# Router logits of an attention and mixture-of-experts block: computed in two column halves of the array, at another place in the order

## Chip, core and metric

One Trainium2 chip, one core. The metric is device time in microseconds (us) of one execution of the whole program, as the median of three runs.

## What is computed

The input is 16 sequences (`b`) of 256 tokens with 256 features, and a context of 256 rows with 192 features for each. First comes cross attention with 16 heads of 64, then a feed-forward layer of 8 experts, each token sent to two of them. Cut to what matters here:

```python
x = x + softmax(q k^T / 8) v @ w_o + b_o             # attention on layernorm(x) and the context
xn = layernorm(x)
logits = xn.astype(float32) @ router_w + router_b    # 256 -> 8, the part that is changed
gates = softmax(logits); two experts per token by top_k
slot = cumsum of the tokens of each expert, cut at a capacity of 640
x = x + sum over a token's experts of gate * expert(xn)   # gelu(xn @ w1 + b1) @ w2 + b2
```

## The kernel before

All engines are programmed by hand. An order that `timeline()` writes out (lines 61 to 146) lists stages such as `("q", n)`. TensorE (PE), ScalarE (ACT), VectorE (DVE) and GpSimd (POOL) each walk this list and run the stages that they own, strictly in its order; semaphores connect them. So moving an entry moves it in every queue that runs it.

The attention part is cut into 64 *periods* `m`, four for each sequence: `b, r = divmod(m, 4)`. Each period handles two pairs of heads. In one period TensorE does, in this order: `scores(m)`; `pv(m-2)`, the product of probabilities and values; `q(m+1)`; `turn0(m-1)`; `k(m+1)`; `turn1`; `v(m)`; `turn2`; `turn3`. The `turn` stages transpose normalised probabilities. Between `turn2` and `turn3` stands what a period has in addition: `o` (output projection) for r = 0, `xt` (transposed input) for r = 1, `x2t` and `o` for r = 2, and `logits` for r = 3. ScalarE runs `exp0`, `exp1`, `a_hi`, `q_hi`, `copy0`, `exp2`, `k_hi`, `copy1`, `exp3`, `copy2`, `v_sb`, `copy3`; `copy0` to `copy3` take the transposed probabilities out of PSUM. VectorE runs `max0` to `max3`, `a_lo`, `inv`/`norm`, `q_lo`, `k_lo` and, between them, the layer norms and the router: `bias`, `shift` and `gate` for r = 0, `rank` for r = 1, `slot` and `keys` for r = 2, `pick` for r = 3. GpSimd scatters the rows after `pick` by four indirect DMAs.

Waits that matter here. `scores(m)` waits for `copy2` of period m-1, which copies probabilities of period m-2 (the semaphore `probt`), and for the exponentials of period m-1. `logits(b)` waits for `x2t_sb(b)`, a copy made at the end of the r = 2 period. Stages that need a PSUM bank for a short time share three banks in turn (`WORKS`, `bank()`): a stage waits until the reader of the stage three entries earlier is done (`WORK_READ`). With `pos` ahead of it that gives `k` of an r = 2 period a wait for `slot` on VectorE. For `logits` the reader is `bias` (semaphore `biased`).

The product that `logits` makes is in float32. The trace shows it as two instructions per matmul: 2 blocks of tokens x 2 blocks of features x 2 = 8 weight loads of 128 columns and 8 matmuls with 8 moving columns. `pv` is float32 as well and writes each head to one half of the PSUM partitions, from weights of 64 columns; `q`, `k`, `v`, `scores` and `o` are float32r products.

In all there are 16 `logits` stages. Thirteen (b = 0 to 12) stand in the r = 3 periods of the main loop, three in the part after it, which is written out singly. After the attention part come 8 experts, which the change does not touch.

Of the kernel before, what the change touches and what calls it, by code (L numbers as in the profile page):

```python
# [27 lines left out]
P = 128  # L28
B, S, D = 16, 256, 256
CD = 192  # L30
HD = 64
# [3 lines left out]
DC = D // P  # L35
NE, HID = 8, 1024
# [23 lines left out]
def timeline():  # L60


    def steps(names, n):
        return [(name, n) for name in names.split()]

    xt, q, k = "xt xt_hi xt_lo", "q q_hi q_lo", "k k_hi k_lo"
    half = ("inv0 norm0 norm1", "inv1 norm2 norm3")
    pv = "pv a_hi a_lo"
    out = steps("ln1_stats ln1_root ctx ln1", 0) + steps("split_hi split_lo", 0) + steps("split_hi split_lo", 1)
    out += [("warm", 28), *steps(xt, 0), ("warm", 8)]  # L70
    out += steps("split_hi split_lo", 2) + steps("split_hi split_lo", 3) + steps(q, 0) + steps(k, 0)
    out += [*steps("q q_hi", 1), ("vsplit", 0), ("ctx", 1), *steps("scores max0 max1 exp0", 0), ("q_lo", 1),
            *steps("max2 max3", 0), ("split_hi", 4), *steps(k, 1), ("exp1", 0), ("split_lo", 4),
            *steps("exp2 exp3 v v_sb", 0), ("split_hi", 5), *steps(half[0], 0)]
    for m in range(1, PERIODS - 2):
        b, r = divmod(m, PER_B)
        out += steps("scores max0 max1 exp0 exp1", m)
        if r == 1 and 3 <= b:
            out += [("rank", b - 3)]
        if r == 1 and 2 <= b:  # L80
            out += [("x2add", ST * (b - 2) + 1)]
        out += [("split_lo", 5)] if m == 1 else []
        out += steps("max2 max3", m)
        out += steps(pv, m - 2) if m >= 2 else []
        if 3 <= b:
            out += {0: [("bias", b - 3)], 2: [("slot", b - 3)]}.get(r, [])
        if r == 1 and 2 <= b:
            out += steps("ln2_stats ln2_root", b - 2) + steps(q, m + 1) + steps(half[1], m - 1)
        else:
            out += steps(half[1], m - 1) + (steps("ln1_stats ln1_root", 1) if m == 1 else []) + steps(q, m + 1)  # L90
        if 3 <= b:
            out += {0: [("shift", b - 3)], 2: [("keys", b - 3)]}.get(r, [])
        out += steps("turn0 copy0", m - 1) + [("exp2", m)] + steps(k, m + 1) + steps(half[0], m)
        out += steps("turn1 copy1", m - 1) + steps("exp3 v", m)
        if r == 0 and b + 1 < B:
            out += [("ctx", b + 1)]
        out += {1: [("vsplit", 1)], 2: [("ln1", 1), ("constants", 0)], 3: [("residual", 0), ("residual", 1)],
                4: [("vsplit", 2)], 5: [("vsplit", 3)]}.get(m, [])
        if 3 <= b:
            out += {0: steps("gate_exp gate", b - 3), 3: steps("pick scatter", b - 3)}.get(r, [])  # L100
        if r == 1 and 2 <= b:
            out += [("ln2", b - 2)]
        if r == 3 and b + 2 < B:
            out += [("ln1", b + 2), ("residual", b + 2)]
        out += [*steps("turn2 copy2", m - 1), ("v_sb", m)]
        if r == (1 if b else 2) and b + 1 < B:
            out += steps(xt, b + 1)
        if r == 2 and 2 <= b:
            out += steps("x2t x2t_sb", b - 2)
        if r == 2 and b + 2 < B:  # L110
            out += steps("ln1_stats ln1_root", b + 2)
        if r == 2 and 1 <= b:
            out += steps("o x2add", ST * (b - 1))
        if r == 0 and 2 <= b:
            out += [("o", ST * (b - 2) + 1)]
        if r == 3 and 2 <= b:
            out += [("logits", b - 2)]
        out += steps("turn3 copy3", m - 1)
        if r == 1 and 3 <= b:
            out += [("pos", b - 3)]  # L120

    c, d, e, m = B - 3, B - 2, B - 1, PERIODS - 2
    out += [*steps("scores max0 max1 exp0 exp1 max2 max3", m), *steps(pv, m - 2), ("slot", c - 1),
            *steps(half[1], m - 1), *steps(q, m + 1), ("keys", c - 1), *steps("turn0 copy0", m - 1), ("exp2", m),
            *steps(k, m + 1), *steps("x2t x2t_sb", c), *steps(half[0], m), *steps("turn1 copy1", m - 1),
            *steps("exp3 v", m), *steps("logits bias shift", c), *steps(half[1], m), *steps("turn2 copy2", m - 1),
            ("v_sb", m), *steps("o", ST * d), *steps("gate_exp gate", c), ("w_hi", 0), ("w_hi", 1),
            ("x2add", ST * d), ("rank", c), *steps("turn3 copy3", m - 1)]
    m += 1
    out += [("w_lo", 0), ("w_lo", 1), *steps("scores max0 max1 exp0 exp1 max2 max3", m), ("pv", m - 2), ("pos", c),  # L130
            ("a_hi", m - 2), *steps("turn0 copy0", m - 1), ("exp2", m), *steps("pick scatter", c - 1),
            ("a_lo", m - 2), *steps("turn1 copy1", m - 1), ("exp3", m), *steps(half[0], m),
            *steps("turn2 copy2", m - 1), *steps("turn3 copy3", m - 1), *steps("v v_sb", m), *steps("slot keys", c),
            *steps("turn0 copy0", m), *steps("turn1 copy1", m), *steps(half[1], m), ("o", ST * d + 1),
            ("pick", c), ("x2add", ST * d + 1), *steps("ln2_stats ln2_root", d), *steps(pv, m - 1),
            *steps("turn2 copy2", m), *steps("turn3 copy3", m), *steps(pv, m), ("ln2", d),
            ("w_hi", 2), ("w_hi", 3), *steps("o x2add", ST * e), *steps("o x2add", ST * e + 1),
            *steps("ln2_stats ln2_root", e), ("scatter", c), *steps("x2t x2t_sb logits", d), ("warm", 14),
            *steps("bias shift gate_exp gate", d), ("ln2", e), ("rank", d), *steps("x2t x2t_sb", e),
            *steps("pos slot keys", d), ("logits", e), ("warm", 18), *steps("bias shift gate_exp", e),  # L140
            *steps("pick scatter", d), *steps("gate rank pos slot keys pick scatter", e),
            ("w_lo", 2), ("w_lo", 3), ("warm", 90)]
    assert len(set(out)) == len(out)
    return out
# [6 lines left out]


TIMELINE = timeline()
WORK_BANKS = 3

# [8 lines left out]
def build(nc, x, ctxt, wq, wk, wv, wo, bo, rw, rb, w1, b1, w2, b2, out):  # L164
    es = ExitStack()
    with es:
        sems = {}

        def sem(name):
            if name not in sems:  # L170
                sems[name] = es.enter_context(nc.semaphore("s_" + name))
            return sems[name]

        def sb(stack, name, shape, dt=F32):
            return stack.enter_context(nc.sbuf_tensor(name, [P, *shape], dt))
# [37 lines left out]
        x2t = sb(rest, "x2t", [DC, S])  # L213
        bo_all = sb(rest, "bo_all", [D])
        rwt = sb(rest, "rwt", [DC, NE])
# [19 lines left out]
        rank, slot, valid, lowkey, highkey = (sb(rest, n, [ST, NE])  # L235
                                              for n in ("rank", "slot", "valid", "lowkey", "highkey"))
# [311 lines left out]
        def _(pe):  # L548
            work = {w: n for n, w in enumerate(WORKS)}

            def bank(stage, n):

                at = work[stage, n]
                if at >= WORK_BANKS:
                    s, m = WORKS[at - WORK_BANKS]
                    pe.wait_ge(sem(WORK_READ[s]), m + 1)
                return psum[:, 5 + at % WORK_BANKS, :]

            def products(dst, terms):
                for j, (lhs, rhs) in enumerate(terms):  # L560
                    mm = pe.matmul(dst, lhs, rhs, start=(j == 0), stop=(j == len(terms) - 1))  # L561
                return mm
# [122 lines left out]
            def logits(b):  # L685
                dst = bank("logits", b)
                pe.wait_ge(sem("x2t_sb"), b + 1)
                for t in range(ST):
                    mm = products(dst[:, t * NE:(t + 1) * NE],
                                  [(x2t[:, k, t * P:(t + 1) * P], rwt[:, k, :]) for k in range(DC)])  # L690
                mm.then_inc(sem("logits"), 1)

            def pos(b):
# [6 lines left out]

            pe.wait_ge(sem("ident"), 1)
            steps = dict(warm=warm, xt=xt, q=q, k=k, v=v_, scores=scores, pv=pv, o=o, x2t=x2t_, logits=logits, pos=pos,
                         turn0=lambda m: turn(m, 0), turn1=lambda m: turn(m, 1), turn2=lambda m: turn(m, 2),
                         turn3=lambda m: turn(m, 3))
# [479 lines left out]
```

## Time and profile before

| | before |
|---|---|
| runs | 1019.17, 1018.17, 1020.28 us; median 1019.17 |
| profiled execution | 1018.17 us, of which the span of the profile is 1016.3 us |
| PE matmul busy | 979.9 us, 96% of the span |
| DVE busy | 769.2 us, 76% |
| ACT busy | 624.3 us, 61% |
| POOL busy | 284.2 us, 28% |
| mean granted clock of TensorE | 0.993 |

The span runs from the first to the last instruction; the rest of the execution, 1.9 us, lies around it. Busy shares are averages over stretches with different limits, and a pipelined engine can count as busy while its order is held up by another.

### The profile page before, as it was taken

How to read it: one execution, taken by the hardware profiler on the slowest of the kernel's cores; microseconds unless marked ns; L12 is line 12 of the kernel's file. 1: busy time of each engine (PE TensorE's matmuls, PEld its weight loads, DVE VectorE, ACT ScalarE, POOL GpSimd, SP SyncE). 2: the span in 40 equal slices, each digit the busy share in tenths (PEclk: the TensorE clock that was granted, in tenths of full speed). 3: DMA queues.
4: the chain of work that ended last, by engine and by line, in shares of the span. 5: the costliest groups of instructions: out<-in, count | busy, mean ns of one | idle time of the engine just before them, and what ended most of it. 6: DMA issues, size and time to landing. Idle time of an engine off the chain costs nothing.

```text
span 1016.3 us, 23196 instructions
## 1 busy us (share of the span) xinstructions
PE 979.9 (96%) x8382; PEld 883.9 (87%) x8382; DVE 769.2 (76%) x2088; ACT 624.3 (61%) x1736; POOL 284.2 (28%) x440
## 2 busy tenths in 40 slices
PE   7889999999999999999999999999888999999996
PEld 6778888888888888888888888888678999999996
DVE  6897768878787888878787887878755666776662
ACT  5777767777776777777676777777514333344330
POOL 5542021314223131313223131311442333222233
PEclk9999999999999999999999999999999999999998
DMA  8440101101010101101010110001105543444522
GB/s 241 144 114 2 33 2 33 43 13 55 14 40 15 33 13 33 44 2 43 12 32 6 33 35 6 17 5 50 58 18 178 137 96 80 113 128 129 136 26 26
DMA packets 48431, 56.74 MB, mean 56 GB/s; under 512 B 5324, under 2 KB 44218, under 8 KB 48192
## 3 DMA queue, kind: packets, MB, share of 16 engines
q1 hardware_dynamic: 39488, 46.30, 14.7%
q0 software_dynamic: 8832, 8.98, 5.5%
q8 instruction: 68, 1.11, 0.5%
q14 instruction: 43, 0.35, 0.1%
HBM read 36.01 MB, written 24.20 MB: 59 GB/s over the span
## 4 chain that ended last, share of the span: by engine, by line
PE 71%; DVE 18%; ACT 5%; issue 4%; DMA 0%; POOLq 0%; POOL 0%; another core or an unknown queue 0%; ACTq 0%
PE psum L561 29%; PE psum L756 11%; PE psum L658 8%; PE psum L644 7%; PE psum L628 7%; PE psum L672 7%; DVE prob L985 5%; ACT prob L819 3%; DVE negmax L974 3%; DVE kl L922 1%; DVE al L922 1%; PE psum L566 1%; DVE stats L929 1%; PE psum L719 1%; DVE ql L963 1%
## 5 line engine op out<-in xcount | busy, mean ns | idle before, releaser
L819 ACT ACTIVATE prob<-psum,negmax 128x256 f32<-128x256 f32 x512 | 239.1, 484 | 81.6 <-DVE negmax L974 81.6
L771 ACT ACTIVATE probt<-psum 128x512 f32<-128x512 f32 x256 | 157.6, 617 | 53.4 <-PE psum L644 51.1
L974 DVE TENSOR_REDUCE negmax<-psum 128x2 f32<-128x512 f32 x256 | 160.0, 683 | 22.0 <-PE psum L628 21.9
L985 DVE TENSOR_SCALAR prob<-prob,invtot 128x256 f32<-128x256 f32 x512 | 168.0, 392 | 4.5
L644 PE MATMUL psum<-ident,prob 128*128 128x128 f32 x1024 | 154.4, 275 | 3.3 <-DVE prob L985 1.7
L644 PEld LDWEIGHTS psum<-ident,prob 128*128 128x128 f32 x1024 | 120.5, 142 | 14.5 <-issue 4.4
L898 ACT ACTIVATE hid<-psum,b1t 128x640 f32<-128x640 f32 x64 | 50.9, 795 | 133.2 <-PE psum L561 133.2
L658 PE MATMUL psum<-probt,v 128*64 128x256 f32 x1024 | 124.6, 385 | 0.8 <-ACT probt L771 0.8
L541 POOL DMA_INDIRECT out_rows<-y,rowi x40 | 65.7, 1644 | 174.5 <-DVE y L1137 169.6
L505 POOL DMA_INDIRECT slot_table<-row,picki x64 | 64.7, 1011 | 170.2 <-DVE picki L1087 143.2
L819 ACT ACTIVATION_READ_ACCUMULATOR prob<-psum,negmax 128x1 f32 x512 | 111.2, 217 | 0.0
L658 PEld LDWEIGHTS psum<-probt,v 128*64 128x64 f32 x1024 | 68.0, 136 | 37.0 <-issue 1.0
L756 PE MATMUL psum<-w2h,hidh 128*128 128x256 f32 x320 | 91.1, 285 | 0.0
L453 POOL TENSOR_SCALAR shifted<-ln_mean_var 128x2 f32<-128x2 f32 x32 | 7.1, 222 | 298.7 <-issue 249.1
L756 PE MATMUL psum<-w2h,hidl 128*128 128x256 f32 x320 | 90.5, 283 | 0.0
L756 PE MATMUL psum<-w2l,hidh 128*128 128x256 f32 x320 | 90.5, 283 | 0.0
L628 PE MATMUL psum<-kh,qh 64*128 64x256 f32 x512 | 80.2, 304 | 5.6 <-ACT probt L771 2.4
L561 PE MATMUL psum<-bufh,w1h 128*128 128x320 f32 x256 | 80.4, 314 | 0.2 <-DVE bufl L922 0.2
L561 PE MATMUL psum<-xth,wqh 128*128 128x256 f32 x256 | 79.0, 309 | 0.5 <-DVE xtl L922 0.5
L561 PE MATMUL psum<-bufh,w1l 128*128 128x320 f32 x256 | 79.1, 309 | 0.0
L561 PE MATMUL psum<-bufl,w1h 128*128 128x320 f32 x256 | 79.1, 309 | 0.0
L672 PE MATMUL psum<-woh,ah 128*128 128x256 f32 x256 | 74.9, 293 | 0.0
(159 smaller groups left out, 2738.4 us busy)
## 6 DMA issues: line engine op xcount, KB each, us to landing
w1r<-in_w SPq DMA_DIRECT2D x8, 1024.0 KB, 8.1
w2r<-in_w SPq DMA_DIRECT2D x8, 1024.0 KB, 10.4
slot_table<-blank SPq DMA_DIRECT2D x8, 662.5 KB, 9.8
rows<-slot_table SPq DMA_DIRECT2D x7, 662.5 KB, 5.4
xin<-in_x SPq DMA_DIRECT2D x16, 256.0 KB, 3.0
out_rows<-x SPq DMA_DIRECT2D x16, 256.0 KB, 3.2
c<-in_ctxt SPq DMA_DIRECT2D x16, 128.0 KB, 3.1
c<-in_ctxt SPq DMA_DIRECT2D x32, 64.0 KB, 2.9
```

Source lines behind the costliest of these rows:

```text
L505: pool.indirect_dma_start(out=table, out_offset=bass.IndirectOffsetOnAxis(ap=picki[:, b % 3, k, t:t + 1], axis=0), in_=row[:, b % 3, t, :] ...
L541: pool.indirect_dma_start(out=out_rows, out_offset=bass.IndirectOffsetOnAxis(ap=rowi[:, e % 2, s:s + 1], axis=0), in_=y[:, e % 2, s, :], i ...
L561: mm = pe.matmul(dst, lhs, rhs, start=(j == 0), stop=(j == len(terms) - 1))
L628: mm = pe.matmul(psum[:, 2 * cc + h, qb * S:(qb + 1) * S], a[r, m % 2, cc, cols], w[r, m % 2, cc, :], start=(j == 0), stop=(j == len(terms ...
L644: mm = pe.transpose(psum[:, TURN_BANK[u], kb * S + qb * P:kb * S + (qb + 1) * P], prob[:, m % 2, u, qb, kb * P:(kb + 1) * P], ident[:, :])
L658: mm = pe.matmul(dst[h * HD:(h + 1) * HD, cc * S:(cc + 1) * S], v[:, b % 2, kb, cols], probt[:, m % 2, 2 * cc + h, kb, :], start=(kb == 0) ...
L672: mm = pe.matmul(dst[:, 0:D], a[:, b % 2, c, tt], w[:, c, :], start=(c == 0 and j == 0), stop=(c == PAIRS - 1 and j == 2))
L756: mm = pe.matmul(dst, a[:, j, ss], w[:, j, :], start=(j == 0 and m == 0), stop=(j == HC - 1 and m == 2))
L771: copy = lambda dst, src, **kw: act.activation(dst, src, ACT.Copy, **kw)
L819: last = act.activation(prob[:, m % 2, u, qb, :], psum[:, u, qb * S:(qb + 1) * S], ACT.Exp, bias=negmax[:, m % 2, u, qb:qb + 1], accum_out ...
L974: dve.tensor_reduce(negmax[:, m % 2, u, :], psum[:, u, :].rearrange("p (q s) -> p q s", q=ST), AX.X, ALU.max, negate=True).then_inc(sem("m ...
L985: last = dve.tensor_scalar(prob[:, m % 2, u, qb, :], prob[:, m % 2, u, qb, :], invtot[:, m % 2, u, qb:qb + 1], None, ALU.mult)
```

## The change

Two things change. First, each 128-token block of `logits` is computed as two column halves of the array: 64 tokens into PSUM partitions 0 to 63 and 64 tokens into 64 to 127, the form that `pv` has. That makes 16 weight loads of 64 columns and 16 matmuls in place of 8 and 8, in all 16 stages. Second, in the r = 3 periods `logits` moves from between `turn2` and `turn3` to directly behind `pv`, and `bias` moves from the next (r = 0) period to behind it. The order of the PSUM banks within these two periods follows.

```diff
         out += steps(pv, m - 2) if m >= 2 else []
+        if r == 3 and 2 <= b:
+            out += [("logits", b - 2)]
         if 3 <= b:
-            out += {0: [("bias", b - 3)], 2: [("slot", b - 3)]}.get(r, [])
+            out += {2: [("slot", b - 3)]}.get(r, [])
+        if r == 3 and 2 <= b:
+            out += [("bias", b - 2)]
...
             out += [("o", ST * (b - 2) + 1)]
-        if r == 3 and 2 <= b:
-            out += [("logits", b - 2)]
         out += steps("turn3 copy3", m - 1)
...
                 for t in range(ST):
-                    mm = products(dst[:, t * NE:(t + 1) * NE],
-                                  [(x2t[:, k, t * P:(t + 1) * P], rwt[:, k, :]) for k in range(DC)])
+                    for k in range(DC):
+                        for h in range(2):
+                            r = slice(h * HD, (h + 1) * HD)
+                            mm = pe.matmul(dst[r, t * NE:(t + 1) * NE], x2t[:, k, t * P + h * HD:t * P + (h + 1) * HD],
+                                           rwt[:, k, :], start=(k == 0), stop=(k == DC - 1))
```

## Rows read from the trace of the kernel before

**Rows 1.** The page: span, and the chain of work that ended last.

```profile
span 1016.3 us, 23196 instructions
...
PE 71%; DVE 18%; ACT 5%; issue 4%; DMA 0%; POOLq 0%; POOL 0%; another core or an unknown queue 0%; ACTq 0%
```

**Rows 2.** Timeline of PE, end of an r = 3 period: start, duration, instruction, count.

```profile
362.89 0.60 PE L644 MATMUL psum<-ident,prob 128*128 128x128 f32 x4
363.33 0.96 PE L561 MATMUL psum<-rwt,x2t 128*128 128x8 f32 x8
364.14 0.63 PE L644 MATMUL psum<-ident,prob 128*128 128x128 f32 x4
364.71 0.38 PE L628 MATMUL psum<-kh,qh 64*128 64x256 f32 x2
```

**Rows 3.** Timeline of ACT in the same period: `a_hi`, `q_hi`, `copy0`, `copy2`.

```profile
358.25 0.60 ACT L771 ACTIVATE ah<-psum 128x512 fp32r<-128x512 f32 x1
359.88 0.60 ACT L771 ACTIVATE qh<-psum 128x512 fp32r<-128x512 f32 x1 [1.03 <-PE psum L561]
360.37 0.59 ACT L771 ACTIVATE probt<-psum 128x512 f32<-128x512 f32 x1
...
363.59 0.65 ACT L771 ACTIVATE probt<-psum 128x512 f32<-128x512 f32 x1
```

**Rows 4.** Groups of weight loads by form: busy us, mean ns | idle before.

```profile
L658 PEld LDWEIGHTS psum<-probt,v 128*64 128x64 f32 x1024 | 68.0, 136 | 37.0 <-issue 1.0
...
L561 PEld LDWEIGHTS psum<-rwt,x2t 128*128 128x128 f32 x128 | 15.9, 195 | 1.2 <-DVE x L1005 1.0
```

**Rows 5.** Timeline of weight loads: the end of `pv`, the start of `q`.

```profile
357.60 0.14 PEld L658 LDWEIGHTS psum<-probt,v 128*64 128x64 f32 x2
358.13 0.19 PEld L561 LDWEIGHTS psum<-xth,wqh 128*128 128x128 f32 x1 [0.39 <-issue]
```

**Rows 6.** Timeline of PE: two neighbouring small matmuls of `pos`.

```profile
341.31 0.17 PE L561 MATMUL psum<-chosen,upto 128*128 128x8 bf16 x1
341.34 0.17 PE L561 MATMUL psum<-before,ones 128*128 128x8 bf16 x1
```

**Rows 7.** Timeline of DVE, r = 3 period: `k_lo`, then the next period's maxima.

```profile
362.39 0.69 DVE L922 TENSOR_TENSOR kl<-psum,kh 128x512 fp32r<-128x512 f32 x1 [0.96 <-ACT kh L771]
...
365.93 2.48 DVE L974 TENSOR_REDUCE negmax<-psum 128x2 f32<-128x512 f32 x4
```

**Rows 8.** Timeline of PE: `logits` of b = 0, 1 and 12.

```profile
137.90 0.96 PE L561 MATMUL psum<-rwt,x2t 128*128 128x8 f32 x8
...
182.59 0.96 PE L561 MATMUL psum<-rwt,x2t 128*128 128x8 f32 x8
...
678.84 0.96 PE L561 MATMUL psum<-rwt,x2t 128*128 128x8 f32 x8
```

**Rows 9.** Waits of PE: released by, us in total, times, longest.

```profile
PE psum L561 <- DVE valid L1062: 2.3, 8, 0.3
```

**Rows 10.** ACT, r = 0 periods: `q_hi` and `k_hi` at 189 us, `q_hi` and `copy0` at 325 us.

```profile
189.20 0.60 ACT L771 ACTIVATE qh<-psum 128x512 fp32r<-128x512 f32 x1 [0.86 <-PE psum L561]
...
191.50 0.60 ACT L771 ACTIVATE kh<-psum 128x512 fp32r<-128x512 f32 x1 [0.31 <-PE psum L561]
...
325.35 0.60 ACT L771 ACTIVATE qh<-psum 128x512 fp32r<-128x512 f32 x1 [1.44 <-PE psum L561]
326.83 0.60 ACT L771 ACTIVATE probt<-psum 128x512 f32<-128x512 f32 x1 [0.88 <-PE psum L644]
```

**Rows 11.** PE, r = 0 period: the last matmul of `q`, and `turn0`.

```profile
324.46 0.28 PE L561 MATMUL psum<-xth,wql 128*128 128x256 f32 x1
324.58 0.60 PE L644 MATMUL psum<-ident,prob 128*128 128x128 f32 x4
```

**Rows 12.** POOL, r = 0 periods: the last of the four scatters, twice.

```profile
189.75 0.97 POOL L505 DMA_INDIRECT slot_table<-row,picki  x1 [0.31 <-issue]
...
325.05 0.99 POOL L505 DMA_INDIRECT slot_table<-row,picki  x1 [0.30 <-issue]
```

**Rows 13.** PE: `logits` of b = 14, after the main loop.

```profile
743.83 1.03 PE L561 MATMUL psum<-rwt,x2t 128*128 128x8 f32 x8 [0.78 <-ACT x2t L771]
```

## The prediction

> **What bounds the kernel now.** I read the page first: of the chain that ended last, 71% lies on TensorE, 18% on VectorE and 5% on ScalarE [rows 1]. The share of PE says that a piece of PE work taken out *can* shorten the time; it does not say that this one does. So I read the timeline of PE around one `logits` stage, then those of ACT and DVE in the same microseconds, then PE's waits, and last the r = 0 period that follows.
>
> PE: `turn2` starts at 362.89, `logits` at 363.33, `turn3` at 364.14, the next `scores` at 364.71 [rows 2]. Thus `logits` costs PE 364.14 - 363.33 = 0.81 us where it stands. The thirteen main-loop stages look alike to 0.01 us, so a change per sequence of d us is 13 d in the sum.
>
> **What the removal frees.** The next `scores` waits for `copy2` on ACT. ACT idles 1.03 us in front of `q_hi`, until PE has finished `q`, and from there works without a gap: `q_hi` at 359.88, `copy0` at 360.37, `copy2` from 363.59 for 0.65 us, to 364.24 [rows 3]. With 0.04 us from end to start, `scores` could not start before 364.28, and did at 364.71. Without `logits` between the turns PE would be ready at 364.71 - 0.81 = 363.90. So of the 0.81 us only 364.71 - 364.28 = 0.43 us can be had; the rest becomes a wait of `scores` for `copy2`. The cover that `logits` had was ACT's own work: before, it stood in a place where PE was only 0.43 us from having to wait anyway.
>
> **What the new place costs.** Behind `pv`, `logits` delays `q` by some x. ACT is idle there, waiting for exactly this `q`, so its whole row of work up to `copy2` starts x later, and so do `k_lo` and what follows it. Per sequence `scores` moves by x - 0.43.
>
> What is x? The form in columns of 64 does not stand in the trace with 8 moving columns. Bounds: today's 8 loads of 128 columns pass in 0.81 us, 0.101 each, and a load of 64 columns takes 136 ns against 195 for 128 columns [rows 4], 59 less, about half of 0.101. The matmuls do not set the pace: small ones of `pos` start 0.03 us apart [rows 6], so sixteen take at most 0.48. If the loads of the two halves go side by side, x = 8 x 0.051 = 0.41; if one by one, x = 16 x 0.051 = 0.81. `pv` has loads of both halves starting at the same hundredth, 357.60, x2 [rows 5]. That is the nearest row, and I take 0.41. The change between 64 and 128 columns in front of `q` is paid today as well, behind `pv`. A gain beyond this (x below 0.41) would need loads faster than any row here. Then d = 0.41 - 0.43 = -0.02, times 13 = -0.3 us. In the main loop the exchange is close to nothing.
>
> The Trainium skill, "TensorE: Matmul & The Clock Gate", section "Part 3: Packing small matmuls", says that weight loads overlap matmuls in flight only when their row group differs. Two column halves share their row groups, so by that rule the sixteen loads would stand in line. By that rule, the trace does not agree: the two loads at 357.60 fall inside the stretch of `pv`'s matmuls.
>
> Edits costed at nothing. `bias` (0.08 us of DVE) moves from r = 0, where DVE idles later in the period, into r = 3, where it stands behind `a_lo` and ahead of a gap of 0.96 us before `k_lo` [rows 7]. It now waits for `logits`, which ends before `a_lo` does, so nothing queues behind that wait. If `logits` came late, `norm2` and `turn2` would be next. The three shared banks: in r = 3, `q` now waits for `x2add`, `k` for `a_lo`, `v` for `bias`; in r = 0, `k` no longer waits for `bias`. All of these readers finish at least 0.3 us before.
>
> **What is shifted after it.** This part carries the forecast. From `k_lo` on DVE runs without a gap to the next `max0` [rows 7], and `pick` stands between them; so `pick`, and POOL's four scatters behind it, move x = 0.41 us later, while PE in the r = 0 period moves by -0.02 only. In r = 0 periods ACT is late against PE today. At 325 us the last matmul of `q` ends at 324.46 + 0.28 = 324.74, `q_hi` starts at 325.35; `turn0` ends at 324.58 + 0.60 = 325.18, `copy0` starts at 326.83 [rows 10, 11]. The late starts fall at 0.30 and 1.78 us after the start of POOL's last scatter, 325.05 [rows 12]. At 189 us that scatter came later against `q`, and there `q_hi` is on time, 0.55 us ahead of the scatter's start, `copy0` too, and only `k_hi` starts 1.75 us behind it [rows 10, 12]. What links POOL and ACT I can't tell from the trace; that the late starts keep this distance is what rows show.
>
> The price of the lateness: a late `copy0` makes `exp2`, `k_hi` and `k_lo` late, then DVE, full from there on, brings `slot` late in the r = 2 period, and `k` on PE waits for it, 8 times, 2.3 us in all [rows 9]. The sequence with the scatter at 189.75 took 182.59 to 227.28 = 44.69 us from one `logits` to the next; all twelve took 678.84 - 137.90 = 540.94, against 12 x 44.69 = 536.28 [rows 8], so 4.66 us of excess. After the change the scatter starts 0.31 + 0.41 + 0.02 = about 0.74 us behind the end of `q`, farther than the 0.59 at 189 us (189.16 to 189.75). So I expect `q_hi` and mostly `copy0` on time, a late start only at `exp2` or `k_hi` at the worst, and the waits of rows 9 gone. Gain: between the 2.3 us recorded as waits and the 4.66 of excess; I take the middle, 3.5.
>
> **The tail.** Of the three stages behind the loop, PE waits in front of that of b = 14 and DVE waits behind it [rows 13]; b = 15 stands the same way. There only the form counts. I take one full 0.4 us on the chain (0.81 - 0.41), between 0 and 0.8.
>
> **Sum.** -0.3 - 3.5 - 0.4 = -4.2 us. Against the profiled execution: span 1016.3 - 4.2 = 1012.1, with the 1.9 us around it 1014.0. The median of the runs is 1.0 above that execution, so 1019.17 - 4.2 = 1015.0.
>
> **Rivals.**
>
> *Nothing moves.* ACT's lateness in r = 0 keeps its place against PE (it would then not hang on POOL), and the exchange is -0.3 - 0.4 = -0.7: 1018.5. For it: `copy0` at 326.83 also coincides with the end of `turn1`. Against: 189 us.
>
> *The lateness moves along with the scatter and still holds `copy0`* (slower). Then `copy0`, `k_hi` and the full DVE chain come 0.41 later in 11 r = 0 periods, and the wait of `k` [rows 9] grows by that: -0.7 + 11 x 0.41 = +3.8, 1023.0. It decides as soon as `copy0`, ready 0.44 us behind `q`'s end, is not released before the hold begins. For it: at 325 us a `q_hi` only 0.31 ahead of the scatter was held; `copy0` would be ready 0.3 ahead of it.
>
> *The column halves stand in line* (slower): x = 0.81, d = +0.38, 13 x 0.38 = +4.9, and no gain in the tail: 1024.1; with the 3.5 us of the forecast also there, 1020.6. For it: nothing here shows loads of a float32 product with so little moving work in between. Against: rows 5. The skill's rule above leads to the same place.
>
> *ACT does not bound `scores`* (the change gives what PE's rows promise): 13 x (0.41 - 0.81) - 0.4 = -5.6, 1013.6; with the relief on top, 1010.1. It needs ACT to start earlier than today although its input comes later; I see no way except that `copy2` is less late than I read.
>
> **How the numbers follow.** Forecast 0.36, nothing moves 0.22, lateness moves along 0.15, halves in line 0.14 (half of it with the relief), ACT no bound 0.10, others 0.03. Within 0.2% (2.0 us, about what a measurement can tell) lie the second case and the relieved half of the fourth: 0.28. Faster: first and fifth, 0.45. Slower: 0.27. The forecast's own range is 1013.5 to 1017, from 2.3 to 4.66 us of relief and the tail's bounds. For 8 in 10 the range takes in the slower cases up to 1023.5 and down to 1012.5; it leaves out most of the fifth case and the end of the fourth.
>
> **What the changed profile would show.** PE idle in front of the r = 3 to r = 0 `scores`, released by ACT's `probt`, about 0.4 us each. `q` starting 0.41 us later behind `pv` (0.81 would be the third rival). ACT idle before `q_hi` in r = 3 of 1.44 instead of 1.03. In r = 0 `q_hi` and `copy0` on time, and rows 9 gone, with sequences near 44.7 us; if they are near 45.5, the lateness moved along. The prediction is wrong if `scores` does not wait, or if the lateness is tied to something else than the scatter.

## The result: slower by 0.3%

| | before | changed |
|---|---|---|
| median of 7 runs each | 1019.17 us | 1022.75 us |
| profiled execution, its span | 1018.17, 1016.3 us | 1023.08, 1021.3 us |
| PE busy | 979.9 us | 975.5 us |

The ratio is 1.0032, with a 95% interval of 1.0018 to 1.0047. The forecast was 1015.0. In later runs (set B below) it was 1.0044 (1.0030 to 1.0058). PE is busy 4.4 us less, and the program takes longer.

The page of the changed kernel, span and chain by engine, answers to [rows 1]: ScalarE went from 5% of the chain to 8%.

```profile
span 1021.3 us, 23452 instructions
...
PE 70%; DVE 14%; ACT 8%; issue 5%; DMA 1%; POOL 0%; POOLq 0%; SPq 0%; ACTq 0%
```

PE's waits, whole span: released by, us in total, times, longest. First the wait of `scores` for `copy2` in the kernel before, then the changed kernel, where 13 of the 17 times, 7.2 us, are the thirteen `scores` behind the r = 3 periods.

```profile
PE psum L628 <- ACT probt L771: 2.4, 4, 0.8
```

```profile
PE psum L630 <- ACT probt L776: 9.6, 17, 0.8
...
PE psum L563 <- DVE valid L1067: 1.5, 5, 0.3
```

Timeline of PE in an r = 3 period, which answers to [rows 2]: end of `pv`, `logits`, `q`, then `turn2` with `turn3`, and `scores`.

```profile
401.92 1.95 PE L660 MATMUL psum<-probt,v 128*64 128x256 f32 x16
403.70 0.59 PE L694 MATMUL psum<-rwt,x2t 128*64 128x8 f32 x16
404.22 0.39 PE L563 MATMUL psum<-xth,wqh 128*128 128x256 f32 x1
...
408.99 1.04 PE L646 MATMUL psum<-ident,prob 128*128 128x128 f32 x8
410.58 0.39 PE L630 MATMUL psum<-kh,qh 64*128 64x256 f32 x2 [0.56 <-ACT probt L776]
```

ScalarE in the same period, which answers to [rows 3]: `q_hi`, `copy0`, and `copy2`.

```profile
405.95 0.60 ACT L776 ACTIVATE qh<-psum 128x512 fp32r<-128x512 f32 x1 [1.44 <-PE psum L563]
406.45 0.59 ACT L776 ACTIVATE probt<-psum 128x512 f32<-128x512 f32 x1
...
409.68 0.65 ACT L776 ACTIVATE probt<-psum 128x512 f32<-128x512 f32 x1
```

From `pv` to `q` it is 404.22 - 401.92 = 2.30 us, against 1.88 without `logits` between them: x = 0.42, as forecast. (x is what `logits` adds in front of `q`.) The sixteen weight loads of 64 columns, 0.14 us each, lie within 0.71 us, beside the end of `pv`:

```profile
403.49 0.71 PEld L694 LDWEIGHTS psum<-rwt,x2t 128*64 128x64 f32 x16
```

ScalarE's idle time before `q_hi` went from 1.03 to 1.44. `scores` waits 0.56 us. But it starts 0.25 us after the end of `copy2` (409.68 + 0.65 = 410.33), not 0.04.

Because the periods repeat, the steps from the first matmul of one `scores` to that of the next say where the time went. Means over the twelve sequences b = 3 to 14, from the PE timelines, us:

| step from r = | 0 | 1 | 2 | 3 | sum over all twelve |
|---|---|---|---|---|---|
| before | 12.09 | 9.93 | 12.98 | 10.07 | 540.93 |
| changed | 12.10 | 10.02 | 12.90 | 10.28 | 543.56 |

The r = 3 period is 0.21 us longer every time, without exception, in thirteen sequences 2.7 us. The other three sum to zero: r = 2 gained 12 x 0.08 = 1.0 us, r = 1 lost 12 x 0.09 = 1.1.

### The profile page after: what moved, and what is told of

It is laid out like the page before. It is cut to its first block, busy times and chain, and to the rows that moved or that the text cites. A ratio compares the mean times of both kernels' runs of the same rounds, so it can differ in the third digit from the quotient of the medians.

```text
span 1021.3 us, 23452 instructions
## 1 busy us (share of the span) xinstructions
PE 975.5 (96%) x8510; PEld 881.6 (86%) x8510; DVE 774.1 (76%) x2088; ACT 623.6 (61%) x1736; POOL 284.1 (28%) x440
## 3 DMA queue, kind: packets, MB, share of 16 engines
q8 instruction: 69, 1.13, 0.5%
## 4 chain that ended last, share of the span: by engine, by line
PE 70%; DVE 14%; ACT 8%; issue 5%; DMA 1%; POOL 0%; POOLq 0%; SPq 0%; ACTq 0%
PE psum L563 26%; PE psum L761 11%; PE psum L660 9%; PE psum L630 8%; PE psum L674 7%; PE psum L646 7%; ACT prob L824 5%; DVE prob L990 4%; ACT probt L776 2%; DVE negmax L979 2%; DVE kl L927 1%; DVE al L927 1%; PE psum L724 1%; PE psum L694 1%; ACT kh L776 1%
## 5 line engine op out<-in xcount | busy, mean ns | idle before, releaser
L646 PE MATMUL psum<-ident,prob 128*128 128x128 f32 x1024 | 151.0, 273 | 5.3 <-DVE prob L990 2.3
L630 PE MATMUL psum<-kl,qh 64*128 64x256 f32 x512 | 75.6, 279 | 0.0
## 6 DMA issues: line engine op xcount, KB each, us to landing
w2r<-in_w SPq DMA_DIRECT2D x8, 1024.0 KB, 10.6
```

Source lines behind the costliest of these rows:

```text
L630: mm = pe.matmul(psum[:, 2 * cc + h, qb * S:(qb + 1) * S], a[r, m % 2, cc, cols], w[r, m % 2, cc, :], start=(j == 0), stop=(j == len(terms ...
L646: mm = pe.transpose(psum[:, TURN_BANK[u], kb * S + qb * P:kb * S + (qb + 1) * P], prob[:, m % 2, u, qb, kb * P:(kb + 1) * P], ident[:, :])
```

## The experiments

The experiments form three sets, A, B and C in order of time ("calls" in the expectations). The kernels of one set ran on one chip, and each ratio is against the kernel before on that chip; medians of different sets don't compare. The last columns are the mean steps of the periods in us. The profiles of sets B and C show ScalarE late in r = 0, as the first one of before did; those of set A don't. This has a part of its own below. The changed kernel itself ran only in set B.

| kernel | ratio, 95% interval | r = 1 | r = 2 | r = 3 |
|---|---|---|---|---|
| *set A, before 1013.59 us* | | | | |
| form alone | 0.9980, 0.9972 to 0.9989 | 9.86 | 12.65 | 9.95 |
| place alone | 1.0105, 1.0091 to 1.0120 | 9.86 | 12.68 | 10.75 |
| `turn2` early | 0.9968, 0.9958 to 0.9979 | 9.87 | 12.84 | 9.66 |
| `ctx` later | 1.0206, 1.0192 to 1.0219 | 9.86 | 14.22 | 10.28 |
| *set B, before 1019.21 us* | | | | |
| before, one run | - | 9.96 | 13.02 | 10.07 |
| changed | 1.0044, 1.0030 to 1.0058 | 10.19 | 12.97 | 10.29 |
| place alone, `turn2` early | 0.9995, 0.9986 to 1.0004 | 9.90 | 12.95 | 10.10 |
| wait last | 0.9986, 0.9977 to 0.9995 | 9.92 | 12.87 | 10.17 |
| *set C, before 1022.63 us* | | | | |
| scatter later | 0.9961, 0.9948 to 0.9975 | 9.92 | 12.66 | 10.28 |
| before, wait last | 0.9991, 0.9982 to 1.0000 | 10.02 | 13.06 | 10.07 |
| `turn2` early | 0.9923, 0.9909 to 0.9936 | 9.94 | 12.96 | 9.66 |
| `turn2` early, wait last | 0.9917, 0.9904 to 0.9931 | 9.87 | 13.03 | 9.66 |

r = 0 stayed within 12.09 to 12.13 in all of them.

In set B the changed kernel lost 4.5 us, 0.44%. There r = 3 took 0.22 us more than in the kernel before, in thirteen sequences 2.9 us, and r = 1 0.23 more, in twelve 2.8; r = 2 gave 0.6 back.

### The form and the place, one at a time

Form alone: the kernel before, with

```diff
-                    mm = products(dst[:, t * NE:(t + 1) * NE],
-                                  [(x2t[:, k, t * P:(t + 1) * P], rwt[:, k, :]) for k in range(DC)])
+                    for k in range(DC):
+                        for h in range(2):
+                            r = slice(h * HD, (h + 1) * HD)
+                            mm = pe.matmul(dst[r, t * NE:(t + 1) * NE], ...
```

> The kernel before with the column halves alone; logits and bias stay where they were, between turn2 and turn3 and in the r = 0 period. Theory (scores of the period after r = 3 waits for copy2 on ScalarE, ready about 0.22 us after that copy's end; the halves cost 0.42 us of PE behind pv and a little more between transposes, whose array form is another): scores comes 0.18 us earlier per sequence, 9.89 instead of 10.07 us for the r = 3 period, in all 13 x 0.18 = 2.3 us faster than before. Rival (PE alone sets the pace): 13 x (0.81 - 0.42) = 5.1 us faster, an r = 3 period of 9.68. Rival (the halves cost as much as the full form outside pv): no change.

Place alone: the changed kernel, with that edit taken back.

> The changed kernel with the full-array form of logits again, so the new place alone. Theory (q and with it all of ScalarE's work up to copy2 is put off by the whole length of logits): the r = 3 period grows from 10.07 to 10.07 + 0.81 - 0.43 + 0.22 = 10.67 us, in all 13 x 0.60 = 7.8 us slower than before. Rival (only PE's total matters): the r = 3 period stays 10.07 and the time within 1 us of before. Rival (what made the change slower is the later GpSimd and VectorE work, not scores): the r = 3 period stays near 10.28.

Timeline of PE, form alone, between `turn2` and `scores`:

```profile
404.83 0.60 PE L644 MATMUL psum<-ident,prob 128*128 128x128 f32 x4
405.36 0.64 PE L692 MATMUL psum<-rwt,x2t 128*64 128x8 f32 x16
405.93 0.66 PE L644 MATMUL psum<-ident,prob 128*128 128x128 f32 x4
406.52 0.39 PE L628 MATMUL psum<-kh,qh 64*128 64x256 f32 x2
```

Timeline of PE, place alone, from `pv` to `q`:

```profile
403.42 1.95 PE L660 MATMUL psum<-probt,v 128*64 128x256 f32 x16
405.30 1.06 PE L563 MATMUL psum<-rwt,x2t 128*128 128x8 f32 x8
406.21 0.36 PE L563 MATMUL psum<-xth,wqh 128*128 128x256 f32 x1
```

Form alone gained 2.0 us, near the 2.3 expected, but not quite by the mechanism that I gave: `scores` doesn't wait there. The halves take 0.57 us (405.36 to 405.93) between transposes of the full array, and `turn2` in front holds 0.53 instead of 0.44 us. Behind `pv` the halves are 0.81 - 0.42 = 0.39 us shorter than the full form was between the turns; in the old place only 10.07 - 9.95 = 0.12 of that is left. Place alone has 406.21 - 403.42 - 1.88 = 0.91 us behind `pv` for x. With the 0.43 us of cover and 0.2 for the start after the wait (0.25 in place of the 0.04 of the prediction), that gives 10.07 + 0.91 - 0.43 + 0.20 = 10.75, which is what was measured (I had expected 10.67, with 0.81 for x). 13 x 0.68 = 8.8 of the 10.6 us of the ratio are the r = 3 periods; the rest I can't place without a profile of before on that chip. The two effects don't add: the form is worth 0.12 in the old place and 0.47 in the new one, where the same half columns stand next to each other.

### Taking the wait for `copy2` away

The changed kernel, `turn2` and `copy2` ahead of `exp3` and `v` in r = 3:

```diff
-        out += steps("turn1 copy1", m - 1) + steps("exp3 v", m)
+        early = r == 3 and 2 <= b
+        out += steps("turn1 copy1", m - 1) + (steps("turn2 copy2", m - 1) if early else []) + steps("exp3 v", m)
...
-        out += [*steps("turn2 copy2", m - 1), ("v_sb", m)]
+        out += ([] if early else steps("turn2 copy2", m - 1)) + [("v_sb", m)]
```

> The changed kernel, with turn2 and copy2 ahead of exp3 and v in the r = 3 periods with logits, so that copy2 ends about 0.9 us earlier while PE does the same work. Theory (scores waits for copy2): that wait goes, the r = 3 period is PE's own work, 10.07 - 0.81 + 0.42 = 9.68 us instead of 10.28, in all 13 x 0.6 = 7.8 us faster than the changed kernel, if the r = 2 and r = 0 periods give none of it back. Rival (scores is held by something else, such as the exponentials or k_lo): r = 3 stays at 10.28 and the time that of the changed kernel. Rival (VectorE is the bound over the four periods): r = 3 shortens, but the waits of k in r = 2 grow by as much, and less than half of the gain stays.

PE's work is the same in amount; only ScalarE's order allows an earlier `copy2`. PE and ACT of this kernel, end of an r = 3 period (`copy1` and `copy2` are the row with x2):

```profile
449.33 0.60 PE L647 MATMUL psum<-ident,prob 128*128 128x128 f32 x4
449.86 0.39 PE L631 MATMUL psum<-kh,qh 64*128 64x256 f32 x2
```

```profile
448.19 1.11 ACT L777 ACTIVATE probt<-psum 128x512 f32<-128x512 f32 x2
449.15 0.52 ACT L825 ACTIVATE prob<-psum,negmax 128x256 f32<-128x256 f32 x1
```

`scores` waits no more; r = 3 takes 9.66 us (9.68 expected), and where the changed kernel lost 0.3% in the result and 0.4% in set B, this one gained 0.3%. The two were not run side by side, so the 7.8 us expected between them were not measured; the r = 3 step is what compares. Of 13 x 0.41 = 5.3 us against before 3.2 us stay. The r = 2 period of this kernel takes 0.19 more than that of form alone on the same chip, 12 x 0.19 = 2.3 us. PE arrives earlier and VectorE does not; 1.0 us of it stands as a wait of `k` for `slot` in the row below. Form alone, with `logits` in its old place, had 0.9980 there against 0.9968, with intervals that overlap: 2.0 of the 3.2 us do not need the new place.

PE's waits in the main loop of this kernel, 120 to 700 us:

```profile
PE psum L564 <- DVE valid L1068: 1.0, 4, 0.3
PE psum L631 <- ACT probt L777: 0.5, 1, 0.5
```

The same step with the full-array form of `logits`:

> logits in the full-array form directly behind pv, with turn2 and copy2 ahead of exp3 and v: the slowest of the places so far, with the wait for copy2 taken away. Theory (the place costs only through that wait; in PE time the two places are nearly equal): an r = 3 period of 10.07 - 0.81 + 0.91 = 10.17 us where place_only had 10.75, in all 13 x 0.10 = 1.3 us slower than before, so 7.5 us faster than place_only. Rival (a late q costs also through k_lo, max0 and what VectorE does after it): more than 3 us slower than before, in longer r = 0 to r = 2 periods.

It gave r = 3 = 10.10 (10.17 expected) where place alone had 10.75. Of the 0.68 us that the place costs over 10.07, 0.65 go when `copy2` runs early. What an early `turn2` does to the kernel before was not run.

### The order of the waits in `scores`

```diff
-                if m >= 2:
-                    pe.wait_ge(sem("probt"), UNITS * (m - 2) + 3)
                 for cc in range(2):
                     if m >= 1:
                         pe.wait_ge(sem("exp"), UNITS * (m - 1) + 2 * (cc + 1))
+                    if m >= 2 and cc == 0:
+                        pe.wait_ge(sem("probt"), UNITS * (m - 2) + 3)
```

> The changed kernel, with the wait for copy2 (semaphore probt) placed last in scores, behind that for the exponentials, instead of ahead of it. It tells where the 0.22 to 0.25 us between copy2's end and the first matmul go, of which I had counted 0.04. Theory (a passed wait behind it costs part of it): the r = 3 period falls from 10.28 to about 10.20, in all 1 us faster than the changed kernel. Rival (it is the way from ScalarE's end to PE's start, or the first weight load that can't run ahead): 10.28 stays, the time too.

ACT (`copy2`) and PE (`scores`) of this kernel:

```profile
409.14 0.65 ACT L776 ACTIVATE probt<-psum 128x512 f32<-128x512 f32 x1
```

```profile
409.94 0.39 PE L630 MATMUL psum<-kh,qh 64*128 64x256 f32 x2 [0.44 <-ACT probt L776]
```

The way from `copy2`'s end to `scores` fell from 0.25 to 409.94 - 409.79 = 0.15 us, and r = 3 from 10.29 to 10.17. So one wait that is passed behind the one that holds costs 0.1 us here. r = 1 steps on time fell from 9.86 to 9.77 as well, but r = 2 steps on time rose from 12.65 to 12.75 and took that back. The whole gain on the changed kernel is larger than the 1 us expected: 0.58% or 5.9 us by the ratios, 7.1 by the medians. r = 3 accounts for 13 x 0.12 = 1.6; the r = 1 and r = 2 periods account for 12 x 0.27 + 12 x 0.10 = 4.4, and these are those that the lateness below makes long. `copy0` is 0.9 us behind `q` in five of the eleven sequences of this kernel, against 2.2 in nine of eleven of the changed one. Why the shift lands well I can't say.

> The kernel before, with the wait for copy2 last in scores: what this costs or brings without the change. Theory: the r = 1 periods take 9.77 instead of 9.86 us and r = 3 stays at 10.07, since scores doesn't wait there; 14 x 0.09 = 1.3 us faster than before, or nothing where VectorE sets the pace and k of r = 2 waits longer instead. Rival (the gain of the changed kernel with this order came with fewer late starts of ScalarE, not from scores): a change of the same 5 to 6 us.

On the kernel before the same edit gave 0.9991, 0.9 us for 1.3 expected, with an interval that just reaches no change, and r = 3 at 10.07. (Its profile is of the slowest of its eleven executions, 1024.69 us.) The 5.9 us are not a property of the edit by itself. And with `turn2` early:

> Both improvements on the changed kernel: turn2 and copy2 ahead of exp3 and v in r = 3, and the wait for copy2 last in scores. Theory (they free different things: the one ScalarE's lateness against scores in r = 3, the other the time that PE spends on passed waits wherever scores has to wait for probt): r = 3 periods 9.65 us, r = 1 periods 9.77 instead of 9.86, in all about 6 to 8 us faster than the changed kernel and the fastest of all, 0.996 or less of before. Rival (once scores does not wait for copy2 in r = 3, the order of its waits is worth nothing): the same as the kernel with turn2 early alone, beside it here.

> The changed kernel with turn2 and copy2 ahead of exp3 and v, again, beside the others of this call and possibly on a chip with ScalarE's lateness in r = 0 (the first one, at 0.9968 of before, showed none). Theory: r = 3 periods of 9.65 us whatever the chip; with the lateness the r = 2 periods take 13.1, so the ratio lies between 0.995 and 0.999. Rival (the gain was that of a chip without lateness): not faster than before on one that has it.

0.9917 and 0.9923 on the same chip, intervals overlapping: once `scores` does not wait in r = 3, the order of its waits is worth nothing that these runs can tell. Both beat the kernel before clearly, and `turn2` early did so on two chips.

### The lateness of ScalarE in r = 0

> The kernel before, unchanged, for a profile on the chip of this call. In the first profile ScalarE started q_hi and copy0 of the r = 0 periods up to 2.1 us after q's end, and sequences took 45.1 us; in the four runs of the first call none did. Theory (the lateness belongs to one chip or one execution, not to the order of the kernel): here q_hi starts 0.04 and copy0 0.54 us after q's end in every r = 0 period, and every sequence takes 44.69 us. Rival (it belongs to this order and the other orders escape it): it is there again.

> The changed kernel, unchanged, beside the others on the chip of this call. Theory (scores waits for copy2): r = 3 periods of 10.28 us against 10.07, which is 13 x 0.21 = 2.7 us slower than before, and r = 1 periods of 9.86 wherever ScalarE is on time. Rival (its loss of 3.3 us came with the lateness of ScalarE on the first chip): the ratio falls to 1.000 here.

It is there again in the kernel before, in set B: at 326.40 `q_hi` starts 0.61 us after `q`'s end (325.51 + 0.28). So it comes back from one execution to the next. It isn't a matter of the order alone either: on the chip of set A none of the four kernels had `q_hi` more than 0.05 us behind `q`, in any sequence, while `turn2` early, one of them, had it 0.7 us late in set C. What is different there I can't say; with one chip for each set, chip and time of running can't be told apart. The expectation that it would be gone was wrong. The chip of set A ran the kernel before in 1013.59 us, 5.6 less than in the result, near the 4.66 us of excess that the prediction read [rows 8]. Its own profile of before wasn't taken.

In the changed kernel the scatter moved against `q`'s end only from 0.31 to 0.50 us, not to 0.74: PE moved 0.21 later too. ACT and POOL, r = 0 period of the changed kernel, `q` ending at 369.47 + 0.28 = 369.75:

```profile
369.82 0.60 ACT L776 ACTIVATE qh<-psum 128x512 fp32r<-128x512 f32 x1 [0.70 <-PE psum L563]
371.27 0.60 ACT L776 ACTIVATE probt<-psum 128x512 f32<-128x512 f32 x1 [0.86 <-PE psum L646]
372.67 0.61 ACT L776 ACTIVATE kh<-psum 128x512 fp32r<-128x512 f32 x1
```

```profile
370.25 0.97 POOL L507 DMA_INDIRECT slot_table<-row,picki  x1 [0.30 <-issue]
```

`q_hi` is on time here and in 7 of the 11 sequences with scatters from b = 5 on, and about 0.75 us late in the other 4. `copy0` is still held in all 11, here until 1.02 us after the scatter's start; in the kernel before it was 1.78, so the late starts do not keep their distance. `k_hi` is 2.9 us after `q` in most sequences instead of 3.5, and three r = 2 periods fell from 13.1 to 12.66. But r = 1 took that back. In set B less came of it: `copy0` of the changed kernel started 2.2 us after `q` in nine of the eleven.

Would the full shift of the forecast, to 0.74 us, have freed `copy0`? Two kernels answer. With the wait last the scatter starts 324.88 - 324.26 = 0.62 us after `q`'s end, where 0.59 went with a punctual `copy0` at 189 us; `q_hi` and `copy0` start 0.14 and 0.89 us after `q`, where 0.04 and 0.53 is on time. PE, ACT and POOL:

```profile
323.98 0.28 PE L563 MATMUL psum<-xth,wql 128*128 128x256 f32 x1
```

```profile
324.40 0.60 ACT L776 ACTIVATE qh<-psum 128x512 fp32r<-128x512 f32 x1 [0.66 <-PE psum L563]
325.15 0.60 ACT L776 ACTIVATE probt<-psum 128x512 f32<-128x512 f32 x1 [0.15 <-PE psum L646]
```

```profile
324.88 0.98 POOL L507 DMA_INDIRECT slot_table<-row,picki  x1 [0.30 <-issue]
```

With `turn2` early in set C it starts 369.03 - 367.90 = 1.13 us after `q`'s end, farther than the forecast's 0.74, and `q_hi` and `copy0` are about 0.7 us late, `copy0` in three sequences 1.0, in all eleven:

```profile
367.62 0.28 PE L564 MATMUL psum<-xth,wql 128*128 128x256 f32 x1
```

```profile
368.61 0.60 ACT L777 ACTIVATE qh<-psum 128x512 fp32r<-128x512 f32 x1 [0.71 <-PE psum L564]
369.10 0.59 ACT L777 ACTIVATE probt<-psum 128x512 f32<-128x512 f32 x1
```

```profile
369.03 0.97 POOL L508 DMA_INDIRECT slot_table<-row,picki  x1 [0.30 <-issue]
```

So the distance of the last scatter from `q` does not decide it. In every profile with the lateness and the scatters in their old place the first sequence with scatters, b = 4 (the one at 189 us), has `q_hi` and `copy0` on time, at distances from 0.58 to 1.43 us. What sets it apart is not known.

To see whether the lateness goes where the scatter goes, the changed kernel with

```diff
-            out += {0: steps("gate_exp gate", b - 3), 3: steps("pick scatter", b - 3)}.get(r, [])
+            out += {0: steps("gate_exp gate", b - 3), 3: steps("pick", b - 3)}.get(r, [])
+        if r == 0 and 4 <= b:
+            out += [("scatter", b - 4)]
```

> The changed kernel, with the four scatters of GpSimd behind ctx in the r = 0 period instead of ahead of residual and ctx; all else as it was. Theory (on the chips that show it, ScalarE is late in r = 0 because its waits for PE fall into the time of the scatters, so the lateness moves with them, off the stretch from q to k_hi): q_hi, copy0 and k_hi of r = 0 start 0.04, 0.53 and 1.91 us after q's end, the r = 1 and r = 2 periods take 9.86 and 12.65 us, r = 3 stays at 10.28. On a chip with the lateness that is 4 to 6 us faster than the changed kernel, which was 1.0032 and 1.0044 of before there; on one without, no change. Rival (the lateness hangs on ScalarE's or PE's own place in the order): q_hi and copy0 stay late.

ACT and POOL, r = 0 period of this kernel; `q` ends at 369.44 + 0.28 = 369.72:

```profile
369.76 0.60 ACT L779 ACTIVATE qh<-psum 128x512 fp32r<-128x512 f32 x1 [0.68 <-PE psum L566]
370.25 0.59 ACT L779 ACTIVATE probt<-psum 128x512 f32<-128x512 f32 x1
371.63 0.62 ACT L779 ACTIVATE kh<-psum 128x512 fp32r<-128x512 f32 x1
```

```profile
371.67 1.10 POOL L510 DMA_INDIRECT slot_table<-row,picki  x1 [0.79 <-POOL c0l L449]
```

This is the first of the four scatters, which now starts 1.95 us after `q`'s end. `q_hi`, `copy0` and `k_hi` start 0.04, 0.53 and 1.91 us after it in all eleven sequences where the scatter was moved; r = 2 is 12.66; and the one r = 0 period where the scatter came early all the same (b = 15 has no `ctx` and no `residual` ahead of it) has `q_hi` 0.88 and `copy0` 2.33 us behind `q`. r = 3 is still 10.28. At 0.9961 the kernel is faster than before although it keeps the whole loss of the change, so on such a chip the lateness costs more than the change. The ratios are 0.7% and 0.8% apart from those of the changed kernel in the result and in set B, more than the 4 to 6 us expected. That the lateness goes with the scatters is shown, where there is one; set A had the scatters in the same place and none. By what path they reach ScalarE's waits is open.

### The long r = 1 periods

POOL and DVE of the changed kernel in the r = 0 to r = 1 stretch of the sequence whose r = 1 step is 10.55:

```profile
377.12 0.74 POOL L445 TENSOR_TENSOR c1s<-c,c1t 64x256 fp32r<-64x256 f32 x1
377.94 0.73 POOL L446 TENSOR_TENSOR c0l<-c,c0h 128x256 fp32r<-128x256 f32 x1
```

```profile
377.25 0.70 DVE L1048 TENSOR_TENSOR above<-gates 128x64 f32<-128x64 f32 x1
377.87 0.21 DVE L1049 TENSOR_TENSOR equal<-gates 128x64 f32<-128x64 f32 x1
378.01 0.75 DVE L1048 TENSOR_TENSOR above<-gates 128x64 f32<-128x64 f32 x1
```

The same `above` takes 0.22 us elsewhere; each of the nine long ones in this kernel ends within 0.1 us of a two-input operation of POOL. PE waits for DVE's `prob` 0.59 us in that period.

But the long comparisons alone do not lengthen r = 1. Form alone has 18 of 32 of them long, both in nine of the twelve sequences, and place alone 20 in ten; their r = 1 steps are 9.86 or 9.87, once 9.89. VectorE of form alone:

```profile
284.14 0.69 DVE L1046 TENSOR_TENSOR above<-gates 128x64 f32<-128x64 f32 x1
284.88 0.75 DVE L1046 TENSOR_TENSOR above<-gates 128x64 f32<-128x64 f32 x1
```

And in set B two of the longest r = 1 steps of the changed kernel, 10.68 and 10.70 in b = 11 and 14, have none. All r = 1 steps above 10.4, in any profile, have a late `copy0`. So the lateness can do it without the comparisons, and the comparisons did nothing without the lateness.

Moving `ctx` away from there:

```diff
-        if r == 0 and b + 1 < B:
+        if r == 1 and b >= 1 and b + 1 < B:
             out += [("ctx", b + 1)]
```

> The changed kernel, with ctx (five GpSimd operations on the next context) in the r = 1 period instead of r = 0, from b = 1 on. Theory of the r = 1 periods (two comparisons of gate on VectorE take 0.7 instead of 0.22 us where a two-input GpSimd operation of ctx runs at the same time, and VectorE has no slack there): all r = 1 periods take 9.87 us, none 10.0 to 10.55, which is 1 to 3 us faster than the changed kernel, if ctx does not meet another stretch without slack. Rival (the long r = 1 periods come from the late start of copy0 alone): they stay, time unchanged.

The kernel became slower, 1.0206, where 1 to 3 us of gain were expected. This chip had no lateness, so nothing was to be gained, and the test can't decide what it was made for. It does show the price: `ctx` now meets the end of r = 1, where `row` (two operations) takes 1.21 us on DVE beside 0.73 before, and `k` waits 17.0 us for `slot`, in 12 sequences.

```profile
391.92 1.82 DVE L990 TENSOR_SCALAR prob<-prob,invtot 128x256 f32<-128x256 f32 x3
393.66 1.21 DVE L943 TENSOR_SCALAR row<-x,ln_mean_var,ln_rstd 128x256 f32<-128x256 f32 x2
```

## Why the prediction was wrong, step by step

*What the removal frees: the mechanism right, its last term mis-sized.* `scores` does wait for `copy2`, and the cover of 0.43 us was read rightly. The step that failed is "with 0.04 us from end to start". I took 0.04 from neighbours such as `k_hi` to `k_lo`; from ACT to PE, with one more wait behind, it is 0.25, of which that wait is 0.1. So d was -0.02 by my sum and +0.21 on the chip; 13 d went from -0.3 to +2.7 us. That is most of the 3.6 us; in set B, with 2.9 us from r = 3, the r = 1 periods took 2.8 besides.

*What the new place costs: right.* x = 0.42 against 0.41. The halves' loads go side by side, and the rival with loads in line (0.81) is out for `logits` too. With it goes, for column halves, the rule of the Trainium skill ("TensorE: Matmul & The Clock Gate", section "Part 3: Packing small matmuls") that the prediction cites, that loads overlap matmuls in flight only when their row group differs: the first of the sixteen loads start at 403.49, in the matmuls of `pv`, which reach to 401.92 + 1.95 = 403.87.

*What is shifted after it: wrong, and the largest term.* I forecast 3.5 us of relief; r = 2 gave 1.0 us back and r = 1 took 1.1. The lateness does hang on the scatter (scatter later). The step that failed is "that the late starts keep this distance": the one sequence at 189 us was taken for the rule. The shift came out at 0.19 us instead of 0.43, because PE moved along by the 0.21 of the first error, and `copy0` stayed held, at 1.02 us behind the scatter and not at 1.78. The full shift would not have been enough either: with the scatter 1.13 us behind `q` instead of 0.74 (`turn2` early, set C) `copy0` was still 0.7 us late. What frees it short of moving the scatters away is open. That the lateness costs time in r = 1 too stood nowhere in the prediction.

*The rival that came closest in time,* 1023.0 for a lateness that moves along, had its condition met, `copy0` not released before the hold, but its sum is right by luck: it asks for longer waits of `k` in r = 2, and the r = 2 periods got shorter (12.98 to 12.90); the loss is the 0.21 us in r = 3.

*The tail: not found.* From `logits` of b = 14 to `pos` of b = 15 it was 755.24 - 743.83 = 11.41 us before and 757.78 - 746.23 = 11.55 after. The span of the profiles grew 5.0 us: 2.2 stand at the last `scores` of the attention part, 2.8 at the first product of the first expert, and the rest, about 2.1, comes behind it, in the experts, which the change does not touch. There the changed kernel's profile has a stretch of 3.4 us with a granted clock of 0.50 (1.2 GHz), from 774.8 us on; just before, PE had waited 1.85 us for the expert's first rows. In the kernel before the last such stretch ahead of the end lies at 749.8, in the tail, and the experts ran at 1.00. First product of the first expert, then granted clock (the third number from the end), before and changed:

```profile
770.64 0.41 PE L561 MATMUL psum<-bufh,w1h 128*128 128x320 f32 x1 [0.16 <-DVE bufl L922]
774.80:778.20 3.40, 3.40 (x27) 3.40 (x25) 2.52 (x5) 1.47 (x3) 0.00 (x0) 1.00 1.04 380
```

```profile
773.46 0.39 PE L563 MATMUL psum<-bufh,w1h 128*128 128x320 f32 x1
774.80:778.20 3.40, 3.40 (x13) 3.40 (x14) 0.59 (x2) 1.48 (x2) 0.00 (x0) 0.50 1.04 394
```

From that product to the end it is 245.7 us before and 247.8 changed. Of the fourteen profiles the five with such a stretch among the experts (of 3.4 us, once 6.8: changed, form alone, place alone, `ctx` later, and before with the wait last) have 247.0 to 247.8, the other nine 245.7 to 246.0. So it comes and goes with the execution, and the 5.0 us of the two profiles overstate the change. The medians differ by 3.6; about 1 us of that lies outside the main loop, and how often each kernel has the stretch is not recorded.

*Sum of the errors.* The forecast was 1022.75 - 1015.0 = 7.8 us off: 3.0 from the start after the wait, 3.5 from the relief, and 1.3 from the tail and what lies behind it. The shares for faster, slower and within 0.2%, too, do not add up from the chances given: these make 0.46, 0.22 (0.25 with the others) and 0.29, not 0.45, 0.27 and 0.28.

*The bias and the banks:* costed at nothing, and no wait in the changed profile belongs to them.

## What to carry to other kernels

Before moving work away from an engine that is busy all the time, look at what that engine would have to wait for next: here 0.43 of 0.81 us was all there was to have, and a new wait also costs the start that follows it, 0.25 us, which a gapless stretch never shows. Then ask what each shift makes later for the producer of that input. Between the turns only the 0.43 us by which PE came later than its input counted, out of 0.81; ahead of the producer's own input `logits` puts off everything by its whole length. What repaired the r = 3 period was to let the late copy run earlier in ScalarE's order. And a pattern read from one sequence out of twelve, as the punctual one at 189 us, needs a second case before it carries a forecast.

## What the runs showed of the hardware that I had not expected

- Sixteen small float32 matmuls in column halves take 0.42 us of PE behind another product in halves and 0.57 between full-array transposes, plus 0.09 more in the transposes ahead; in the full form 0.91 behind `pv` and 0.81 between transposes. For the halves that makes an estimate of (0.57 + 0.09 - 0.42) / 2 = 0.12 us for each of the two changes of the array's form. It does not cover the full form, which meets one such change in front of `q` in either place and still takes 0.10 longer behind `pv`.
- A wait on PE that is passed, behind one that holds, delayed the first matmul by 0.1 us (0.25 to 0.15). It shortened r = 3 and moved 0.1 us from r = 1 to r = 2.
- ScalarE's waits for PE ended up to 2.1 us late while four indirect DMAs were issued by GpSimd, in sets B and C and the first two profiles, and not in set A; with the scatters put elsewhere the stretch was on time.
- A stretch of 3.4 us, once 6.8, at a granted clock of 0.50 (1.2 GHz) at the start of the experts goes with 247.0 to 247.8 us from their first product to the end, in five profiles, against 245.7 to 246.0 in nine.
- A comparison of VectorE that ran beside a two-input operation of GpSimd took 0.69 to 0.76 us instead of 0.22, and left the r = 1 step at 9.86 or 9.87 where `copy0` was on time.
